# An adapted residual layer on one core: order of the first loads, the low-rank product in rounded parts, and one bank of tile 1 in rounded parts

## The reference

```python
# x [32, 64, 512], w0 [200, 64, 64], W [512, 512], A [8, 16, 512], Bm [8, 512, 16], all float32
x = x + einsum('bct,bcd->bdt', x, w0[i0])                  # layer 0: own 64x64 matrix of each sample
H = einsum('btd,od->bto', x, W)                            # layer 1: shared 512x512 matrix
xa = einsum('btd,brd->btr', x, A[i1])                      # low rank of the sample's adapter (16)
x = x + H + einsum('btr,bor->bto', xa, Bm[i1]) * scalings[i1][:, None, None]
```

## Time and profile before

| | |
|---|---|
| median of three runs | 83.15 us (82.30 to 85.71) |
| profiled execution, its own time | 83.01 us |
| its span, first to last instruction | 81.3 us |
| TensorE busy | 74.2 us, 91% |
| VectorE / ScalarE / GpSimd busy | 51.6 / 47.6 / 35.7 us |
| DMA | 14.58 MB, mean 179 GB/s |
| matmul instructions | 482 |

### The profile page before, as it was taken

One profiled execution on the slowest core, in us unless ns is written; L12 is line 12 of the kernel. 1 busy time (PEld: TensorE's weight loads), 2 busy tenths in 40 slices (PEclk: granted clock), 3 DMA queues, 4 the chain that ended last, 5 costly groups with the idle time before them and its releaser, 6 DMA issues.

```text
span 81.3 us, 1928 instructions
## 1 busy us (share of the span) xinstructions
PE 74.2 (91%) x482; PEld 67.8 (83%) x482; DVE 51.6 (63%) x125; ACT 47.6 (59%) x105; POOL 35.7 (44%) x76
## 2 busy tenths in 40 slices
PE   4999299999498999999999999999999999999950
PEld 4975288975396999999999999999999999999940
DVE  3830689150797958684868486948694878548730
ACT  0730696431988929292939394848575757375540
POOL 4200068999847653554455454465355523000000
PEclk9999999999999999999999999999999999999999
DMA  0899655589999879777897879668815452303015
GB/s 0 238 356 225 237 156 108 143 214 194 175 194 224 221 213 235 256 268 189 266 247 220 149 241 250 227 128 265 219 61 130 146 172 79 129 0 129 8 58 204
DMA packets 13198, 14.58 MB, mean 179 GB/s; under 512 B 6786, under 2 KB 8066, under 8 KB 13186
## 3 DMA queue, kind: packets, MB, share of 16 engines
q1 hardware_dynamic: 7714, 9.32, 37.5%
q0 software_dynamic: 4640, 4.23, 25.3%
q10 hardware_dynamic: 832, 0.91, 4.0%
HBM read 10.23 MB, written 4.19 MB: 177 GB/s over the span
## 4 chain that ended last, share of the span: by engine, by line
PE 65%; DMA 16%; DVE 5%; issue 5%; ACT 3%; POOL 2%; POOLq 0%; ACTq 0%
PE z_ps L566 45%; DMA scale_sb<-scales 8%; DMA b_raw<-b_t 8%; PE out_ps L601 4%; PE out_ps L619 4%; PE v_ps L595 4%; PE out_ps L615 4%; PE out_ps L614 4%; ACT w_raw L304 1%; ACT b_high L332 1%; DVE moving L438 1%; DVE b_stack L465 1%; DVE a_table L502 1%; POOL w_sb L248 1%; ACT moving L295 1%
## 5 line engine op out<-in xcount | busy, mean ns | idle before, releaser
L566 PE MATMUL z_ps<-moving,x_high 128*128 128x272 f32 x224 | 33.4, 290 | 0.0
L566 PEld LDWEIGHTS z_ps<-moving,x_high 128*128 128x128 f32 x224 | 30.8, 188 | 1.2
L240 POOL DMA_DIRECT2D b_raw<-b_t x32 | 19.6, 615 | 13.7 <-DMA w_raw<-w_t 8.1
L566 PE MATMUL z_ps<-moving,x_low 128*128 128x272 f32 x112 | 18.6, 288 | 0.0
L316 ACT ACTIVATE z_high<-z_ps 128x240 fp32r<-128x240 f32 (+1 forms) x28 | 10.7, 384 | 11.6 <-DVE low_rank L478 11.4
L233 POOL CAST moving<-a_table 128x128 fp32r x28 | 8.7, 340 | 17.4 <-PE z_ps L566 16.8
L456 DVE TENSOR_TENSOR z_low<-z_ps,z_high 128x240 fp32r<-128x240 f32 (+1 forms) x28 | 11.8, 422 | 6.9 <-ACT z_high L316 6.9
L566 PEld LDWEIGHTS z_ps<-moving,x_low 128*128 128x128 f32 x112 | 15.9, 189 | 0.0
L465 DVE TENSOR_TENSOR b_stack<-b_raw,b_high 128x512 fp32r<-128x512 f32 x16 | 11.1, 695 | 5.1 <-ACT b_high L332 4.4
L332 ACT ACTIVATE b_high<-b_raw,low_rows 128x512 fp32r<-128x512 f32 x16 | 11.5, 716 | 2.8 <-DMA b_raw<-b_t 2.8
L431 DVE TENSOR_TENSOR x_low<-x_raw,x_high 128x512 fp32r<-128x512 f32 x14 | 10.6, 754 | 0.0
(11 more groups left out here) (47 smaller groups left out, 62.6 us busy)
## 6 DMA issues: line engine op xcount, KB each, us to landing
x_raw<-xt SPq DMA_DIRECT2D x16, 256.0 KB, 5.5
b_raw<-b_t POOLq DMA_DIRECT2D x32, 128.0 KB, 4.8
out<-out_sb SPq DMA_DIRECT2D x15, 256.0 KB, 4.1
w_sb<-w SPq DMA_DIRECT2D x32, 16.0 KB, 4.0
w_raw<-w_t ACTq DMA_DIRECT2D x1, 272.0 KB, 3.4
w_raw<-w_t SPq DMA_DIRECT2D x1, 272.0 KB, 4.5
a_raw<-a_t ACTq DMA_DIRECT2D x1, 256.0 KB, 4.2
w_raw<-w_t ACTq DMA_DIRECT2D x1, 240.0 KB, 6.8
```

The lines of the kernel that those rows point to most:

```text
L240: pool.dma_start(b_raw[s * C:(s + 1) * C, t % BBUFS, :], b_t[ds(which[s], 1), :, :].to_broadcast([GROUPS, RANK, OUT]),).then_inc(b_loaded[ ...
L566: last = nc.tensor.matmul(z_bank(t, part), x[:, t % XBUFS, k * P:(k + 1) * P], moving[:, int(n == HL), k, at:at + HALF], start=((n, k) == ...
```

## The change

- **Loads.** The two W pieces of column half 0 change places (rows 256 to 511 first) and are both issued by ScalarE's queue, so A becomes its third transfer and W piece (columns 272 on, rows 0 to 255) its fourth. SyncE loads x of tile 0 in two halves, the half that goes with rows 256 to 511 first.
- **Scalings.** They travel behind the indices in one array (`heads`). A one-row matmul with ones spreads them over 128 partitions in PSUM, VectorE copies them to `scale_sb`. The broadcast DMA is gone.
- **Warm-up.** 4 matmuls, the scaling matmul, 1 more, in place of 8.
- **Clearing.** GpSimd clears `w0_sb` in place of VectorE.
- **Tile 1's W bank** is 12 rounded products in place of 4 plain ones. It waits for all four high parts of W, then for all four low parts; x of tile 1 is split too. Its A bank stays plain.
- **Low rank in parts, tiles 2 to 15.** VectorE takes the two own 32-column blocks, ScalarE writes the rounded high part in three groups, VectorE the low part in the fourth. One rounded matmul of 256 columns (high and low of w0) replaces the plain one of 128. VectorE then needs two instructions for `v_stack`. ScalarE writes the high part of w0 instead of VectorE.
- **Orders.** `weigh_low_rank(t)` stands behind layer 0 of tile t-1; `load_b(1)` stands ahead of `take_a(2)`; the ScalarE and VectorE lists change as below.

```diff
-    WARM_UP = 8
+    WARM_UP = (4, 1)
-    PIECES = [(cols, rows) for cols in ((0, HALF), (HALF, OUT)) for rows in ((0, K // 2), (K // 2, K))]
+    UPPER, LOWER = (0, K // 2), (K // 2, K)
+    PIECES = (((0, HALF), LOWER), ((0, HALF), UPPER), ((HALF, OUT), UPPER), ((HALF, OUT), LOWER))
-    ADDED = (2, 3, 0, 5)
+    ADDED = (1, 3, 0, 5)
+    FIRST_ROWS = (K - 1, *range(K // 2, K - 1), *range(0, K // 2))
@@ sync
-            load_x(0)
-            load_w(1)
+            sync.dma_start(x_raw[:, 0, half:], xt[0, :, half:]).then_inc(x0_lower_loaded, 16)
+            sync.dma_start(x_raw[:, 0, 0:half], xt[0, :, 0:half]).then_inc(x_loaded[0], 16)
             load_x(1)
             load_w(3)
@@ gpsimd
-            pool.dma_start(scale_sb[:], scales...to_broadcast([P, ADAPTERS])).then_inc(scales_loaded, 16)
+            nc.gpsimd.memset(w0_sb[:], 0.0).then_inc(w0_cleared, 1)
             load_b(which[0], 0)
+            load_b(which[1], 1)
             pool.wait_ge(a_ready, 1)
             take_a(which[2], 2)
-            load_b(which[1], 1)
@@ scalar
             load_w(0)
+            load_w(1)
             act.dma_start(a_raw[:], a_t).then_inc(a_loaded, 16)
             load_w(2)
+            def high_of_w0(i):
+                act.wait_ge(w0_added, i + 1)
+                nc.scalar.activation(w0_parts[:, first:end, 0, :], w0_sb[:, first:end, :], ACT.Copy).then_inc(w0_high_ready, 1)
+            def high_of_low_rank(t):
+                act.wait_ge(low_rank_ready, t - PLAIN + 1)
+                nc.scalar.activation(low_rank_parts[:, t % 2, :, 0:LOW_U, :], each, ACT.Copy).then_inc(rank_high_ready, 1)
             high_of_w(0)
+            high_of_w(1)
-            high_of_w(1)
-            take_z(0, W_PART)
+            high_of_x(1)
             high_of_w(2)
+            take_z(0, W_PART)
             high_of_w(3)
+            high_of_x(2)
             take_z(1, A_PART)
-            high_of_x(2)
             take_z(0, A_PART)
+            high_of_b(0)
             take_z(1, W_PART)
+            high_of_x(3)
             high_of_v(0)
+            high_of_low_rank(2)
             high_of_b(1)
             high_of_v(1)
             high_of_z(2, A_PART)
+            high_of_w0(BATCH_OF[2])
             high_of_x(4)
             high_of_v(2)
             high_of_b(2)
@@ scalar, t = 3 to 14
                 high_of_z(t - 1, W_PART)
                 high_of_x(t + 2)
+                high_of_low_rank(t)
                 high_of_z(t, A_PART)
+                high_of_b(t)
                 high_of_v(t)
-                high_of_b(t)
                 take_out(t - 1)
+                if t % 2:
+                    high_of_w0(BATCH_OF[t + 1])
@@ vector
+                    nc.vector.tensor_tensor(out=own_low_rank[:], in0=u..., in1=own_rank[:, :, 0, :], op=ALU.mult)
+            def low_of_low_rank(t): ...
+                    nc.vector.scalar_tensor_tensor(out=v_stack[:, t % 2, :], in0=v_ps[t % 2][:, P:2 * P],
+                                                   scalar=group_sb[:, LOW_V:LOW_V + 1], in1=v_rest[:], ...)
+            dve.wait_ge(scales_done, 1)
+            nc.vector.tensor_copy(scale_sb[:], v_ps[0][:, 0:ADAPTERS]).then_inc(scales_ready, 1)
             add_diagonal(0), (1), (2)
+            low_of_w(0)
             a_scaled
-            low_of_w(0)
             low_of_w(1)
-            add_diagonal(3), (4)
+            low_of_x(1)
             low part of a_table
+            add_diagonal(3), (4)
+            low_of_w(2)
             take_low_rank(1)
-            low_of_w(2)
             low_of_w(3)
+            low_of_x(2)
             take_low_rank(0)
@@ tensor
+            nc.tensor.matmul(v_ps[0][:, 0:ADAPTERS], warm[0:1, :], index_sb[... scalings].bitcast(fp32), ...)
-            plain_products(1, W_PART, range(K)).then_inc(w_bank_done, 1)
-            pe.wait_ge(w_low_ready, len(PIECES))
+            pe.wait_ge(w_high_ready, len(PIECES))
+            products(1, W_PART, PRODUCTS[0:2 * K])
+            pe.wait_ge(w_low_ready, len(PIECES))
+            products(1, W_PART, PRODUCTS[2 * K:]).then_inc(w_bank_done, 1)
             a_bank(2)
...
+                    nc.tensor.matmul(v_ps[t % 2][:, 0:2 * P], low_rank_parts[:, t % 2]..., w0_parts[:, t]...)
             for t in range(3, last):
                 a_bank(t)
                 w_bank(t, 0, 2 * K)
-                weigh_low_rank(t)
                 whole_layer0(t - 1)
+                weigh_low_rank(t)
                 w_bank(t, 2 * K, 3 * K)
```

More of the change, by code:

```diff
@@ L156, in read_indices @@
             _, values = nc.values_load_multi_w_load_instructions(
-                index_sb[0:1, kind, PER * t:PER * (t + tiles)], engines=(eng.engine,), min_val=0, max_val=count - 1)
+                index_sb[0:1, PER * (TILES * kind + t):PER * (TILES * kind + t + tiles)], engines=(eng.engine,), min_val=0, max_val=count - 1)
             return [values[PER * i:PER * (i + 1)] for i in range(tiles)]
@@ L346, in high_of_v @@
                 nc.scalar.activation(v_high[:, t % 2, :], v_ps[t % 2][:, 0:P], ACT.Copy,
-                                     scale=low_groups[:, 0:1]).then_inc(v_high_ready, 1)
+                                     scale=group_sb[:, LOW_V:LOW_V + 1]).then_inc(v_high_ready, 1)
+            def high_of_w0(i):
+                first, end = BATCHES[i]
+                act.wait_ge(w0_added, i + 1)
+                nc.scalar.activation(w0_parts[:, first:end, 0, :], w0_sb[:, first:end, :],
+                                     ACT.Copy).then_inc(w0_high_ready, 1)
+            def high_of_low_rank(t):
+                act.wait_ge(low_rank_ready, t - PLAIN + 1)
+                if t >= PLAIN + 2:
+                    act.wait_ge(v_done, t - 1)
+                each = own_low_rank[:].rearrange("p s (g r) -> p s g r", g=1).to_broadcast([P, PER, LOW_U, RANK])
+                nc.scalar.activation(low_rank_parts[:, t % 2, :, 0:LOW_U, :], each, ACT.Copy).then_inc(rank_high_ready, 1)
             def take_out(t):
@@ L407, in _ @@
             nc.vector.memset(warm[:], 1.0).then_inc(warm_ready, 1)
[L408 to L420, removed]
             def add_diagonal(i):
@@ L440, in low_of_w, with low_of_w0 @@
                                         op=ALU.subtract).then_inc(w_low_ready, 1)
-            def split_w0(i):
+            def low_of_w0(i):
                 first, end = BATCHES[i]
-                dve.wait_ge(w0_added, i + 1)
-                nc.vector.tensor_copy(w0_high[:, first:end, :], w0_sb[:, first:end, :]).then_inc(w0_high_ready, 1)
                 dve.wait_ge(w0_high_ready, i - BATCH_OF[PLAIN] + 1)
-                nc.vector.tensor_tensor(out=w0_low[:, first:end, :], in0=w0_sb[:, first:end, :],
-                                        in1=w0_high[:, first:end, :].bitcast(fp32),
+                nc.vector.tensor_tensor(out=w0_parts[:, first:end, 1, :], in0=w0_sb[:, first:end, :],
+                                        in1=w0_parts[:, first:end, 0, :].bitcast(fp32),
                                         op=ALU.subtract).then_inc(w0_low_ready, 1)
@@ L551, in plain_products @@
                 at = FIRST[t % 2] + bank_of(t, part) * HALF
-                for k in ks:
+                for n, k in ks:
                     last = nc.tensor.matmul(z_bank(t, part), x_raw[:, t, k * P:(k + 1) * P],
-                                            w_raw[:, k, at:at + HALF], start=(k == 0), stop=(k == K - 1))
+                                            w_raw[:, k, at:at + HALF], start=(n == 0), stop=(n == K - 1))
                 return last
@@ L618, in layer0 @@
                     pe.wait_ge(z_low_ready[part], t - PLAIN + 1)
-                return nc.tensor.matmul(dst, w0_high[:, t, :], z_low[:, t % 2, col:col + n], start=False, stop=True)
+                return nc.tensor.matmul(dst, w0_parts[:, t, 0, :], z_low[:, t % 2, col:col + n], start=False, stop=True)
             def whole_layer0(t):
@@ L623, in whole_layer0, with warm_up @@
                 layer0(t, out_ps[t % 2][:], 0, OUT, (A_PART, W_PART)).then_inc(out_done, 1)
+            def warm_up(n):
+                for _ in range(n):
+                    nc.tensor.matmul(v_ps[1][:, 0:P], warm[:], warm[:], start=True, stop=True)
             pe.wait_ge(warm_ready, 1)
-            for _ in range(WARM_UP):
-                nc.tensor.matmul(v_ps[1][:, 0:P], warm[:], warm[:], start=True, stop=True)
+            warm_up(WARM_UP[0])
+            pe.wait_ge(index_loaded, 16)
+            nc.tensor.matmul(v_ps[0][:, 0:ADAPTERS], warm[0:1, :],
+                             index_sb[0:1, 2 * TILES * PER:2 * TILES * PER + ADAPTERS].bitcast(fp32),
+                             start=True, stop=True).then_inc(scales_done, 1)
@@ L629, in _ @@
+            warm_up(WARM_UP[1])
+            in_turn = list(enumerate(FIRST_ROWS))
+            by_row = list(enumerate(range(K)))
+            pe.wait_ge(x0_lower_loaded, 16)
+            pe.wait_ge(w_loaded[0], 16)
+            plain_products(0, W_PART, in_turn[:1])
+            pe.wait_ge(w_diag, ADDED[0])
```

(3 more changed lines are left out.)

148 lines of the change are left out of this document (92 added, 56 removed).

## The result

The changed kernel took 80.38 us in the median of four executions (80.14 to 80.53), the kernel before 83.12 (82.30 to 85.71): ratio 0.969, interval 0.963 to 0.976. That is 2.7 us less where 4.1 were forecast, 80.38 in place of 78.9, inside the stated range of 77.4 to 81.0 but outside the forecast's own of 77.4 to 79.8. A few executions fall in a slower state; the ratios are worked out from the fast ones alone and lie up to 0.8% beside the quotient of the medians.

What follows compares the result with a forecast made beforehand. TensorE was taken to bound the kernel from 30 us on, with two DMAs on the chain before 26 us. Terms -1.7 - 1.3 + 0.2 - 1.4 + 0.1 = -4.1 from 83.0 gave 78.9 us, range 77.4 to 81.0.

Steps and rivals of the forecast that it cites:

- step 3: From A's landing to `a_bank(2)`: VectorE's list decides, start at 13.3 instead of 15.02; -1.7 us, between -0.5 and -2.1.
- step 4: B tables before 26 us: earlier issues remove most stalls, layer 0 of tile 2 near 22.5; -1.3 us, between 0 and -1.6.
- Step 1: Start-up scalings without a DMA: the broadcast halved DMA pace, costing some 0.8 us for everything landing behind.
- Step 2: Moved loads: A, now third in ScalarE's queue, lands at 7.5 (ends 6.9 and 8.7); x of tile 1 about 6.5.
- The 8.7: Rival for A's load: lands at 8.7 like its queue's old third transfer, shifting 1.2 us to 80.1; chance 0.15.
- Step 5: B of tile 3: its issue moves by 2 us only, TensorE by over 3; +0.2 us, between 0 and 1.
- Step 6: Low-rank weighing: rounded matmul takes 0.12 us, saving 0.10 in each of 14 tiles; -1.4 us, period 4.06.
- the short cover: Weighing of tile 15: no layer 0 stands between to hide its new chain; +0.1 us, between 0 and 0.3.
- Rival A: Start-up: shorter warm-up makes the clock rise late, `a_bank(2)` comes 1.3 us later, 80.2 us; chance 0.1.
- Rival C: First 26 us: DMA engines are the bound, layer 0 of tile 2 only 1 us sooner, 80.7 us; chance 0.17.
- Rival D: Steady tiles: the chain through ScalarE sets the period, slower, 84.9 us; chance 0.04.
- Rival E: No gain: something taken for hidden sets the first 26 us, rounded weighing costs like plain, 82.5 us; chance 0.06.

Runs made afterwards that it cites:

- z4: Changed kernel with B tables spread, tile 0's parts of B behind in the lists, and 4 and 4 warm-ups: 78.79 us (0.952).
- z1: Changed kernel with B of tile 0 issued after W piece 1, tile 1 after piece 3, tile 3 earlier, tile 0's parts behind: 79.09 us (0.956).
- y1: Changed kernel with B of tiles 0 to 2 issued after W piece 1, B of tile 3 earlier, tile 0's parts behind: 79.89 us (0.960).
- x4: Changed kernel with GpSimd issuing B of tiles 0 and 1 after W piece 1 instead of W piece 3: 79.60 us (0.952).
- y2: Kernel before with only the scalings changed: sent behind the indices, spread by a one-row matmul, no broadcast DMA: 81.67 us (0.980).
- z2: Changed kernel with 4 and 4 warm-up matmuls instead of 4 and 1, B order unchanged: 80.58 us (0.972).

## Why the prediction was right in kind and its gain 1.4 us too large

The spans of the two profiled executions are 81.34 and 78.85, a difference of 2.5 us, where the sum said 4.1. That 80.38 lies in the stated range owes something to luck: the range reaches beyond 79.8 only for the rivals, and of the two large terms for the first 26 us, step 3 came out by another path than the one worked out and step 4 did not come at all.

- **Step 1, right.** The DMA pace at 5.8 to 7.5 us rose from 189 to 382 GB/s, and to 333 with this part alone. ScalarE no longer waited for the scalings. That part gave 1.25 us by itself.
- **Step 2, right.** 7.5 was taken for A's landing. It came at 6.3 in the first profile and at 7.1 to 7.6 in the ten others of this queue order. The rule of the Trainium skill ("DMA: Bandwidth & Descriptors", Queues, rings and completion order), that each engine takes turns between the queue rows, fits in so far as both rows progress together. The 8.7 that the working tied to it was the landing of the old third transfer, and the run with the scalings alone has that at 8.0: a part of it had been the broadcast.
- **Step 3, right in size (-1.5 us for -1.7), wrong in its path.** The working let VectorE's list decide. That list was done at 12.0, and TensorE had no gap from 4.47 to the wait at tile 0: its own instructions decided. For these the working had 8.1 + 3.6 + 0.8 = 12.5 and left out the 1.5 us of tile 1's rounded bank, with which it is 14.0; the 0.8 us of waiting did not come, and the bank took 1.7. In the eleven profiles of the changed queue order `a_bank(2)` starts at 13.5 to 13.9 where the pace of the plain products doubled by 8.5 us, and at 14.3 to 14.9 where it doubled at 10 or later.
- **Step 4 failed.** It said that "earlier issues find room" and left 0.3 of 1.6 us. By the waits before 26 us, 1.38 + 0.19 after stand against 1.2 + 0.4 before: **0.0 instead of -1.3**. The work between was forecast well (8.9, measured 23.92 - 13.54 - 1.57 = 8.8), the waits were not. B of tile 1 came 3.1 us sooner and its stall went as forecast, but another of the same size stood at tile 0, which I had not followed as a term because its B was in time before. TensorE now needed it sooner, and it came no sooner: the first 4 KB packets of B moved at 12.2 (12.0 before), 3.0 us after the first issue where it had been 1.4. And `high_of_b(0)` ahead of four other steps made ScalarE hold these too.
- **Why B of tile 0 took 5.7 us is not shown.** I had blamed `load_b(1)` directly behind `load_b(0)`. For it: issued near 6.6, the second half took 4.2 and 4.8 us with nothing behind it (z4, z1) and 6.4 and 6.7 with another B table directly behind (y1, x4). Against it as the only cause: with B of tile 1 apart (y2) it still took 6.4, and with it directly behind, issued near 10, anything from 4.4 to 5.7.
- **Step 5, mis-sized in this profile:** +0.6 instead of +0.2. Layer 0 of tile 2 came 1.93 us sooner than before and that of tile 4, by the same count, 1.58, although two cheaper weighings lie between. In the second profile of the same kernel this stall was absent, which is also the 0.6 us by which the two spans differ (78.9 and 78.3).
- **Step 6, right:** 4.165 to 4.05, 14 x 0.115 = -1.6 for -1.4. Doubled, it cost the same again. At tile 15 the short cover showed: 0.20 in place of 0.12, **+0.1**.
- **Sum:** -1.5 + 0.0 + 0.6 - 1.6 + 0.1 = -2.4, for 2.5 measured.
- **Rival A happened and cost nothing here.** The pace doubled at 8.4 us, in the second profile near 10, and in the ten profiles with five warm-ups anywhere from 7 to 10.7; in the four with eight at 7.3, 7.6, and by 5.5 and 6.0. I had 1.3 us for it, because I had `a_bank(2)` decide. It did move that mark, to 14.5 in the second profile; the wait behind it took it all.
- **Rival C comes nearest in size (80.7), and half of its mechanism is there.** It had x4 and B of tiles 2 and 3 landing nearly when they did. x4 (19.5 for 19.6) and B of tile 3 did; B of tile 2 came 2.8 us sooner, and layer 0 of tile 2 came 1.9 us sooner, not 1. The runs narrow it: each transfer moved ahead made another late, but the engines' pace is not the bound as such, since with B spread they were busy for 0.55 and 0.58 of the time at 10 to 16 us (z1, z4), and the kernel was some 1.5 us faster than z2 with the old order beside it.
- **Rival D** is excluded by the period, in which TensorE has no wait. **Rival E** by the first and the last part of the sum.

## What to carry to other kernels

When a stall goes, follow each transfer of the same queue to its landing, also those that were in time: the wait moves to the one with the least slack, and a list in order makes everything behind it late too. A half idle DMA stretch is no promise that a transfer issued into it lands sooner: look at its first bytes as well as at its issue, and try the order with one transfer moved at a time. A tiny broadcast can be the dearest transfer of a start-up: look at the pace of the engines around it, not at its size.

## What was not expected of the hardware

The page grants the full clock (1.00) in all windows, yet plain products of 272 columns run at 0.45 us per instruction (1.2 GHz) until 5.5 to 10.7 us and at 0.23 (2.4 GHz) after. With the same code the rise came at 8.4 in one execution and near 10 in another. The pace of the instructions, not the clock column, shows it. And 4 KB of scalings, spread to 128 partitions by GpSimd's queue, cost the DMA engines about half their pace for 1.7 us: 189 and 206 GB/s in the two profiles with it, 333 and 382 without. Its 16 packets of 256 bytes ran in just that stretch and held an engine for up to 0.94 us each, where a packet of 2 KB at 3.7 to 4.9 us took 0.084. What slowed the rest is open.
